# Perceiver with three streamed cross-attentions: key fills in two halves a head, the first layer's queries in the projection, weights layer by layer

## The reference

```python
q = (query @ Wq + bq).reshape(B, Nq, H, D).transpose(0, 2, 1, 3)
k = (key_value @ Wk + bk).reshape(B, Nkv, H, D).transpose(0, 2, 1, 3)
v = (key_value @ Wv + bv).reshape(B, Nkv, H, D).transpose(0, 2, 1, 3)
attn = jnp.einsum('bhqd,bhkd->bhqk', q, k) * scale
attn = jax.nn.softmax(attn, axis=-1)
x = jnp.einsum('bhqk,bhkd->bqhd', attn, v).reshape(B, Nq, Cq)
return x @ Wo + bo
```

## Time and profile before

| | us |
|---|---|
| median of three runs | 3258.68 |
| the profiled execution | 3258.21 |
| its span, first to last instruction | 3256.3 |
| TensorE busy | 2891.9 (89%) |
| VectorE busy | 1842.6 (57%) |
| ScalarE busy | 1345.5 (41%) |
| GpSimd busy | 402.9 (12%) |
| mean granted TensorE clock | 0.916 of full |

### The profile page before, as it was taken

How to read it: one execution, slowest core, us unless ns; L and a number is a source line. 1 busy time by engine, 2 the same in 40 slices (tenths; PEclk the granted TensorE clock), 3 DMA queues, 4 the chain that set the end, 5 groups by cost and what they waited for, 6 DMA issues and landing times. The chain is left out here.

```text
span 3256.3 us, 67384 instructions
## 1 busy us (share of the span) xinstructions
PE 2891.9 (89%) x27158; PEld 2423.6 (74%) x27158; DVE 1842.6 (57%) x3246; ACT 1345.5 (41%) x2191; POOL 402.9 (12%) x571
## 2 busy tenths in 40 slices
PE   7999669996869996769998769999999999999978
PEld 6999636664846665646665656999999999999867
DVE  5666457774348773548874524555555555555424
ACT  4555327663017763216765201444444444444311
POOL 2444300001000000000000005020202021100000
PEclk9999869997869997779998866999999999999969
DMA  5788756561756562366653451110101010000016
GB/s 160 292 329 316 302 146 170 167 168 39 275 145 171 168 172 69 118 163 176 169 171 95 153 151 51 29 41 1 40 1 40 1 40 1 1 1 1 17 53 234
DMA packets 211364, 394.10 MB, mean 121 GB/s; under 512 B 40077, under 2 KB 171534, under 8 KB 208363
## 3 DMA queue, kind: packets, MB, share of 16 engines
q1 hardware_dynamic: 203182, 386.99, 38.0%
q10 hardware_dynamic: 7872, 2.77, 0.4%
HBM read 290.13 MB, written 99.52 MB: 120 GB/s over the span
## 5 line engine op out<-in xcount | busy, mean ns | idle before, releaser
L757 DVE TENSOR_REDUCE L_xattn_tops<-psum 128x1 f32<-128x896 f32 x672 | 702.7, 1087 | 235.7 <-PE psum L603 234.2
L680 ACT ACTIVATE L_xattn_probs<-psum 128x512 f32<-128x512 f32 x1176 | 618.0, 599 | 421.2 <-PE psum L616 418.7
L1746 DVE TENSOR_SCALAR_CACHE_REDUCE L_units_raw<-psum 128x448 f32<-128x448 f32 x448 | 277.6, 620 | 460.4 <-PE psum L1662 457.8
L603 PE MATMUL psum<-L_xattn_keys,L_xattn_q_stack 96*128 96x448 bf16 (+1 forms) x1344 | 392.8, 377 | 98.8 <-DMA L_xattn_keys<-key_parts 51.2
L1706 ACT ACTIVATE L_units_raw<-L_units_raw,L_units_negmax 128x896 f32<-128x896 f32 x224 | 221.7, 1037 | 591.7 <-DVE L_units_negmax L1756 591.7
L1682 PE MATMUL psum<-wide_tokens,L_units_high 128*128 128x386 f32 x1568 | 456.2, 358 | 1.4 <-DVE L_units_low L1765 1.4
L616 PEld LDWEIGHTS psum<-L_xattn_q_stack,L_xattn_keys 99*128 99x128 bf16 (+1 forms) x4704 | 307.1, 99 | 181.4 <-issue 83.7
L616 PE MATMUL psum<-L_xattn_q_stack,L_xattn_keys 99*128 99x128 bf16 (+1 forms) x4704 | 406.8, 222 | 11.3 <-POOL L_xattn_q_stack L725 7.1
L1683 PE MATMUL psum<-wide_tokens,L_units_low 128*128 128x194 f32 x1568 | 395.1, 252 | 0.0
L631 PE MATMUL psum<-L_xattn_probs,L_xattn_values 128*17 128x128 f32 x9408 | 330.8, 277 | 0.4 <-ACT L_xattn_probs L680 0.4
L1682 PEld LDWEIGHTS psum<-wide_tokens,L_units_high 128*128 128x128 f32 x1568 | 294.7, 188 | 11.4 <-DVE L_units_low L1765 1.6
(11 more groups left out here) (436 smaller groups left out, 3981.3 us busy)
## 6 DMA issues: line engine op xcount, KB each, us to landing
L_xattn_keys<-key_parts SPq DMA_DIRECT2D x864, 112.0 KB, 2.7
key_parts<-proj_parts SPq DMA_DIRECT2D x84, 672.0 KB, 5.2
...
```

Of the source, the lines that this page charges most:

```text
L603: last = pe.matmul(top_slot(n)[:, s, :], q_stack[0:P1, h, :], keys[0:P1, v % RING, key:key + WIN // 2], start=True, stop=True)
L680: act.activation(group_probs(k), score_bank(k), ACT.Exp).then_inc(sem("probs"), 1)
L757: dve.tensor_reduce(tops[:, h % 2, 2 * c + w:2 * c + w + 1], top_slot(n), AX.XY, ALU.max)\
L1746: dve.tensor_scalar(raw[u % 2][:, s * SUB:s * SUB + width], bank(g, s % 2, 0, width), 0.0, None, ALU.add, ALU.max, accum_out=tops[:, h, s: ...
```

## The change

Key and value fills from the second head on are made in two parts of four and three slots (`HALVES`); the first head keeps pairs (`FIRST`). Its values are filled by ScalarE. `LEAD` is 9 instead of 10, and `turn_max` stands between the two reductions of a head's first unit instead of after its second unit. Layer 0's normalization and queries move into the projection: the matmuls stand after the second key tile, the parts lie in a buffer that the values use later. Layer 0's stage reads them back at once, fills ones and mask for 14 slots, and waits only for the stores of layer 0's key parts before the first head's fills; the wait for all stores, the last seven slots' ones and mask stand before the third head. `wq` and `bq` are shared buffers from x0 on, and the output stages of layers 0 and 1 load the next layer's. The projection loads, rounds and splits its weights layer by layer; the first half chunk does all key tiles and then all value tiles. The last 64 rows of a weight are loaded into both halves of the partitions by one DMA.

```diff
-        LOADS = 16 * (6 * NL + 4)
+        LOADS = [16 * (4 + (2 if l else 0)) for l in range(NL)]
...
+            def load_weights(l, which):
+                cols = slice(l * D, l * D + D)
+                for w, name in which:
+                    sp.dma_start(w_a[:, w, cols], a[f"L{l}_xattn_{name}"][0:128, :]).then_inc(sem(f"weights{l}"), 16)
+                    sp.dma_start(w_b[:, w, cols], dram(a[f"L{l}_xattn_{name}"], 128 * D, [[0, 2], [D, C1], [1, D]]))\
+                      .then_inc(sem(f"weights{l}"), 16)
...
-            for l in range(NL):
-                cols = slice(l * D, l * D + D)
-                for w, name in ((0, "Wk"), (1, "Wv")):
-                    sp.dma_start(w_a[:, w, cols], a[f"L{l}_xattn_{name}"][0:128, :]).then_inc(sem("weights"), 16)
+            load_weights(0, ((1, "Wv"),))
+            for l in range(1, NL):
+                load_weights(l, ((0, "Wk"), (1, "Wv")))
             load(1)
...
+            norm_tensor(pe, g, st)
             pe.wait_ge(sem("some"), 1)
-            pe.matmul(bank(g, 7, 0, 1), g.ones[:], some[:], start=True, stop=True).then_inc(sem("mask_count"), 1)
-            pe.wait_ge(sem("weight_parts"), 4)
+            pe.matmul(bank(g, 6, 0, 1), g.ones[:], some[:], start=True, stop=True).then_inc(sem("mask_count"), 1)
+            pe.wait_ge(sem("split"), 2)
+            for n in range(NK2):
+                pe.wait_ge(sem("weight_parts"), 2 * (n // DG + 1))
+                key_tile(0, n)
+                if n == 1:
+                    pe.wait_ge(sem("wq"), 16)
+                    pe.wait_ge(sem("xnT"), 1)
+                    for k in range(DG):
+                        for j in range(DG):
+                            last = pe.matmul(bank(g, 4, k * T, k * T + T), wq[:, j, k * 128:k * 128 + 128],
+                                             g.xnT[:, j, :], start=(j == 0), stop=(j == DG - 1), skip_group_check=True)
+                    last.then_inc(sem("q_in_psum"), 1)
+            pe.wait_ge(sem("q"), 1)
             pe.wait_ge(sem("drop"), 1)
-            for i in range(NH - 2):
+            for t in range(GT):
+                value_tile(0, t)
+            pe.wait_ge(sem("value_in_psum"), GT)
+            for i in range(1, NH - 2):
                 pe.wait_ge(sem("split"), 2 * (i + 1))
                 for n in range(NK2):
                     key_tile(i, n)
...
+            act.dma_start(w_a[:, 0, 0:D], a["L0_xattn_Wk"][0:128, :]).then_inc(sem("weights0"), 16)
+            act.dma_start(w_b[:, 0, 0:D], dram(a["L0_xattn_Wk"], 128 * D, [[0, 2], [D, C1], [1, D]]))\
+               .then_inc(sem("weights0"), 16)
+            act.dma_start(wq, a["L0_xattn_Wq"].rearrange("(k p) n -> p k n", p=128)).then_inc(sem("wq"), 16)
+            for l in range(1, NL):
+                for k in range(DG):
+                    act.dma_start(bk[:, l, k:k + 1], dram(a[f"L{l}_xattn_bk"], 128 * k, [[1, 128], [1, 1]]))\
+                       .then_inc(sem(f"weights{l}"), 16)
             round_context(0)
-            act.wait_ge(sem("weights"), LOADS)
-            act.copy(wh_a[:], w_a[:]).then_inc(sem("weights_rounded"), 1)
-            act.copy(wh_b[:], w_b[:]).then_inc(sem("weights_rounded"), 1)
-            round_context(1)
+            round_weights(0)
             act.wait_ge(sem("bk_zero"), 1)
-            for i in range(NH):
+            for n in range(NK2):
+                high(n)
+                if n > 0:
+                    middle(n - 1)
+                if n < NL - 1:
+                    round_weights(n + 1)
+                if n == 2:
+                    act.wait_ge(sem("qparts"), 1)
+                    act.dma_start(dram(g.query_parts, 0, [[T, 128], [D * T, 3], [128 * T, DG], [1, T]]),
+                                  qparts.rearrange("p i (k t) -> p i k t", k=DG)).then_inc(written("query_out"), 16)
+                if n == 3:
+                    round_context(1)
+            round_context(2)
+            for i in range(1, NH):
...
+            def query():
+                dve.wait_ge(sem("q_in_psum"), 1)
+                dve.wait_ge(sem("any_key"), 1)
+                dve.tensor_scalar(q, bank(g, 4, 0, D), g.any_key[:], HD ** -0.5, ALU.mult, ALU.mult).then_inc(sem("q"), 1)
+                dve.wait_ge(sem("q"), 1)
+                link(dve.tensor_copy(qparts[:, 0, :], q))
+                link(dve.tensor_tensor(qrest, q, qparts[:, 0, :], ALU.subtract))
+                link(dve.tensor_copy(qparts[:, 1, :], qrest))
+                dve.tensor_tensor(qparts[:, 2, :], qrest, qparts[:, 1, :], ALU.subtract).then_inc(sem("qparts"), 1)
 
...
+            low_context(0)
+            low_weights(0)
+            dve.wait_ge(sem("bk_zero"), 1)
+            dve.wait_ge(sem("ones"), 1)
+            for n in range(NK2):
+                key_rest(0, n)
+                if n < NL - 1:
+                    low_weights(n + 1)
+                if n == 1:
+                    query()
+                if n == 3:
+                    low_context(1)
+            for t in range(GT):
+                take_value(0, t)
+            low_context(2)
+            dve.wait_ge(written("query_out"), 16)
+            dve.memset(values[1][:, :, :, HD:VW], 1.0).then_inc(sem("ones"), 1)
+            dve.wait_ge(sem("ones"), 2)
+            for i in range(1, NH - 2):
                 for n in range(NK2):
                     key_rest(i, n)
                     take_value(i, n)
...
-    LEAD = 10
...
-    PAIRS = [(c, min(2, NCH - c)) for c in range(0, NCH, 2)]
+    FIRST, HALVES = ((0, 2), (2, 2), (4, 2), (6, 1)), ((0, 4), (4, 3))
+
+    def groups(h):
+        return HALVES if h else FIRST
+
+    def fills(h):
+
+        return h // DEEP + (1 if h % DEEP else 0) if h else 1
...
-            def ones_rows(eng):
-                eng.dma_start(keys[SEG:SEG + 3, :, :], dram(g.ones_row, 0, [[0, 3], [0, RING], [1, CH]]))\
-                   .then_inc(sem("key_rows"), 16)
...
+            def mask_rows(eng, slot, landed):
+                eng.dma_start(keys[SEG + 3:SEG + 4, slot:slot + NCH, :],
+                              dram(g.mask_row, 0, [[NK, 1], [CH, NCH], [1, CH]])).then_inc(landed, 16)
+
+            def drained(eng):
+                for r in range(PARTS_RING):
...
                 if masked:
-                    for r in range(PARTS_RING):
-                        sp.wait_ge(g.drain.sem(f"parts_out{r}"), 16 * 2 * NCH)
-                    for r in range(2):
-                        sp.wait_ge(g.drain.sem(f"values_out{r}"), 16 * 3 * len(range(r, NCH, 2)))
+                    sp.wait_ge(g.drain.sem("query_out"), 16)
+                    for row in range(3):
+                        stack_rows(sp, row)
                     sp.wait_ge(g.drain.sem("mask_out"), 16)
-                if masked:
-                    ones_rows(sp)
-                    for p in range(DEEP):
-                        sp.dma_start(keys[SEG + 3:SEG + 4, p * NCH:p * NCH + NCH, :],
-                                     dram(g.mask_row, 0, [[NK, 1], [CH, NCH], [1, CH]])).then_inc(sem("mask_rows"), 16)
+                    ones_rows(sp, 0, 2 * NCH, sem("key_rows"))
+                    for p in range(2):
+                        mask_rows(sp, p * NCH, sem("mask_rows"))
                     sp.wait_ge(sem("stack_zero"), 1)
                     sp.dma_start(q_stack[SEG + 3:SEG + 4, :, :],
                                  g.ones_bf[0:1, :].unsqueeze(1).to_broadcast([1, H, T]))\
                       .then_inc(sem("stack"), 16)
-                fill_keys(0, 0)
-                sp.wait_ge(sem("qparts_out"), 16)
-                for row in range(3):
-                    stack_rows(sp, row)
-                sp.wait_ge(sem("stack"), STACK)
-                for j in range(1, len(PAIRS)):
-                    fill_keys(0, j)
-                if not masked:
-                    ones_rows(sp)
+                    for c, n in groups(0):
+                        for r in range(DG):
+                            sp.wait_ge(g.drain.sem(f"parts_out{r}"), 16 * 2 * (c + n))
+                        fill_keys(0, c, n)
+                else:
+                    for c, n in groups(0)[:2]:
+                        fill_keys(0, c, n)
+                    sp.wait_ge(sem("qparts_out"), 16)
+                    for row in range(3):
+                        stack_rows(sp, row)
+                    sp.wait_ge(sem("stack"), STACK)
+                    for c, n in groups(0)[2:]:
+                        fill_keys(0, c, n)
+                    ones_rows(sp, 0, RING, sem("key_rows"))
                 for h in range(1, H + 1):
-                    for j, (c, n) in enumerate(PAIRS):
+                    if masked and h == 2:
+                        drained(sp)
+                        ones_rows(sp, 2 * NCH, NCH, sem("late_rows"))
+                        mask_rows(sp, 2 * NCH, sem("late_rows"))
+                    for c, n in HALVES:
                         if h < H:
                             if h >= DEEP:
```

(48 more changed lines are left out.)

138 lines of the change are left out of this document (65 added, 73 removed).

## The result

The changed kernel takes 3212.07 us (median of 4 runs, 3202.59 to 3221.14), the one before 3259.20 on the same chip: a ratio of 0.9856, 95% interval 0.9826 to 0.9887, 47.1 us saved where 53.7 were predicted.

What follows compares the result with a forecast made beforehand. TensorE bounds the streamed stages inside, but SyncE's key-fill issues had become slower, so keys came late. 31.0 + 12.8 + 4.5 + 5.4 + 0 = 53.7 us off 3258.7 gives 3205 us, range 3190 to 3220 (0.70).

Steps and rivals of the forecast that it cites:

- the 35.0 us of surplus: Streamed stages of layers 0, 1 and 2: heads take 19.3, 7.5 and 8.2 us more than at TensorE's pace.
- The 31.0: Key fills in two halves: waits for keys between heads go, 17.3 + 6.5 + 7.2 us; bounds 0 and 35.
- A: Stalls between heads stay, as four-chunk issues take twice as long or DMA engines are the limit: 3236 us, chance 0.10.
- B: Projection: new weight loads as slow as the row of ones, first half chunk some 30 us later: 3235, chance 0.08.
- C: Streamed stages: a half's first top waits for all four chunks, which land late: slower, 3312 us, chance 0.04.
- the starts: Starts of the three streamed stages: 12.8, 4.5 and 5.4 us gained in layers 0, 1 and 2.
- The earlier transpose of the maximum: May save the 0.3 us stops in front of a head's first scores; counted as nothing, at most 5 us.
- Start of layer 0, 12.8: Queries' round trip gone, fewer ones and mask rows: scores 13.4 us earlier, 0.6 paid back; bounds 5 and 20.
- two thirds are 8: Layer 0's start: ones and mask rows for 14 slots instead of 21 take 8 us instead of 12.
- Starts of layers 1 and 2, 9.9: Query weights already there, fewer issues and units before the scores: 4.5 and 5.4 us; bounds 3 and 25 together.
- Rival D: The starts gain nothing, as the row of ones sets them; only the fills' 31.0 us: 3228 us, chance 0.08.
- The projection, 0: First half chunk ends between 4.0 us sooner and 3.1 later; the middle, 0, taken; bounds -4 and +4.

Runs made afterwards that it cites:

- in the second: The changed kernel run and profiled once more with no edit: 3209.00 us, 0.9861 to the kernel before.

## Why the prediction was right, and where it was not

The time lies 7 us from the forecast and inside its own range. The mechanism named first holds: SyncE's issues set the heads' pace. An issue costs the same for four chunks as for one or two, the queue got its pauses, and the 35.0 us of surplus went, all of it, in the kernel before with halves alone. The 31.0 were 4.0 short of that. Rivals A, B and C are out: no stop between heads, the first half chunk 4.7 us later and not 30, no half landing late.

That the total is so near is luck. The forecast is 31.0 us for the fills and 22.7 for the starts. By the times the fills alone bring 27 us, the transposition, counted as nothing, 18.6 (11 to 26), and the edits to the projection, the queries and their weights together nothing that shows (under some 7 us). The transposition stands in for the starts.

Four steps failed.

- *"The earlier transpose of the maximum ... I count nothing, at most 5 in all."* In the changed kernel it is 18.6 us (11 to 26), the period falling from 18.1 to 17.9 us, which is 7.3 us in the two profiles, and 7 more at the starts and ends of the attentions. I priced it by the profile of before, where the wait of 7.1 us stood in the page, but where SyncE and not TensorE set most heads. Priced there it is indeed nothing (1.0006). The step to take was to ask what is late once SyncE is not.
- *Start of layer 0, 12.8.* Head 1's maximum came 6.5 us sooner. Tops began at 423.5 instead of the 418.3 forecast. The term that failed is "two thirds are 8" with the keys 4 us behind: with ones and mask rows for 14 slots and not 21, issued 2.2 us sooner (404.18 for 406.35), the last of the first six key transfers landed at 423.4, where before it had landed at 422.4 (411.4 and 11.0 us). The keys came no sooner at all. So of the round trip that was taken away no more than 4.4 us could be won, from these keys to the tops at 426.85. Part of it is the projection, which ended 3.1 us later (the stage begins at 395.5 instead of 392.4): where the split weight loads let it end 4.4 us sooner, tops begin 4.5 us sooner than here. From tops to the scores were 19.5 us, as forecast (19.0), for 23.8 before.
- *Starts of layers 1 and 2, 9.9.* The table has 1.0 and -0.4. Up to the first scores the forecast for layer 1 came true: from the query matmuls they take 39.0 us for 42.8, and 1.25 us of the wait in front are gone, 5.1 together; layer 2 has 5.1 too. It is what follows that was sized wrong. The unit moved among the scores was to cost 0.6 us, but from the first scores to head 1's maximum pass 14.1 us instead of 12.2, and 15.1 instead of 11.6 in layer 2. And the stages in between took 2 us longer each, which differs from profile to profile (0.6 and 1.3 in the second). Loading the weights a stage ahead gives nothing (0.9841 without, 0.9861 with): I took 1.4 us for a wait that lies in front of a stop of 9.5, and a stop swallows what comes before it. That stop, the ones rows in front of the keys, was where the time was: it went when they did. Rival D, that the starts gain nothing, held in sum for these two layers, within the table's 3 us, and not for layer 0; its 3228 missed because of the transposition.
- *The projection, 0.* Its first matmul came at 19.08 (17.5 forecast), and the half chunk ended 4.7 us later, at 56.45. I gave the middle between two ends that were both worked out from a mechanism, where the trace of the ones rows already leaned to one. The rule of the Trainium skill that I set beside it ("DMA: Bandwidth & Descriptors", same section) says two engines, and with two engines I had estimated -3.1. The window with 0.20 of the engines busy, some three of sixteen with all other traffic, and the half chunk's 4.2 us with split loads agree with it; no run shows how many carried the load. But the other end, 47.8 "if the weights land in time", was wrong as well: with split loads the half chunk ends at 52.27. TensorE still stops 4.08 us before the fifth tile, where I had 2.2, and a pair of matmuls then takes 0.95 us instead of 0.57 at the lower clock, a term that I had at nothing.

One term was in nobody's sum: 8.4 us behind layer 2, in stages that the diff leaves alone. Together, in the profiles: 15.6 us too much in the starts and 8.4 behind layer 2, against 11.4 more than forecast in the heads and 2.7 behind them, of which the transposition has its share. The total came out near because these cancel.
